# One transformer-like block on one core: Q/K rounding split, router steps, dt products, share of the C products on GpSimd, and new instruction orders

## The chip, the core and the metric

The kernel runs on one core of a Trainium2 chip. The core has TensorE (PE, matrix products, with its weight load shown apart as PEld), VectorE (DVE), ScalarE (ACT), GpSimd (POOL) and SyncE (SP, which here only issues transfers). Each engine takes its instructions strictly in the order in which they are written, and waits for another engine by a semaphore. The metric is the device time in microseconds; of the kernel before it is 5525.69 us, the median of 3 runs (5523.0 to 5528.63).

## The reference

32 batches of 512 tokens with 256 features go through an adaptive layer norm, a block, a second adaptive layer norm and a mixture of low-rank experts:

```python
h = layernorm(x) * (1 + ca) + sa
xn = ln(h, ln1);  q, k, v = xn @ q_w + q_b, xn @ k_w + k_b, xn @ v_w + v_b      # 16 heads of 16
attn_out = softmax(causal(q k^T / 4)) v @ o_w + o_b
x_ssm, z = split(xn @ in_proj_w)                                               # 512 and 512 features
x_c = silu(conv4(x_ssm) + conv_b);  dt_raw, Bm, Cm = split(x_c @ x_proj_w)      # 16, 16, 16
dt = softplus(dt_raw @ dt_w + dt_b)
# over t, for each of 512 channels and 16 states:  h = exp(dt*A)*h + (x_c*dt)*Bm ;  y = sum(Cm*h)
ssm_out = ((y + x_c*D_param) * silu(z)) @ ssm_out_w
x1 = h + a*attn_out + (1-a)*ssm_out;  x1 = x1 + gelu(ln(x1, ln2) @ ffn_w1 + b1) @ ffn_w2 + b2
x = x + ga * x1
h = layernorm(x) * (1 + cb) + sb
logits = h @ router_w.T + router_b                                             # 8 experts, the best 2 kept
w = softmax(where(logits < second_best, -1e9, logits))
x = x + gb * (h @ base_w.T + base_b + 2 * sum_e w_e * (h @ lora_A_e) @ lora_B_e)
```

## The kernel before, in words

One batch is one turn of a loop. In a turn each engine runs a list of named steps, and the five lists (ORDER, one for each engine) are written out by hand. A name with + belongs to the next batch, one with - to the batch before, so that three batches overlap. PLACE gives to each product of TensorE one of four PSUM banks (pM0 to pM3). A bank is filled again only when its last reader has signalled.

**The scan.** A batch has 64 scans (e = 0 to 63) of 128 channels by 512 tokens, in 32 pairs k. For each pair GpSimd writes x_c\*dt\*B into two of eight slots of `state` (step fill*k*, L575). ScalarE writes exp(dt\*A) into one of two PSUM banks pD (dec*e*, L714). VectorE scans (scan*e*, L1207). Then the result is multiplied by C: 48 of the 64 products on VectorE (c*e*, L1215, which reads pD and writes `state`), 16 on GpSimd (pc*e*, L563, which reads and writes `state`; for those the scan writes `state` instead of pD). The list POOL_C names the 16: both scans of each fourth pair. TensorE adds the product, transposed, into pY (add*e*, L945), and that frees the slot for a later fill. The rows of B and C come by transfers of SyncE (rb*k*, rc*k*) into four slots of `bc`; a row's transfer starts when the last reader of its slot has signalled.

**Attention.** TensorE makes scores (mx, L1033 and L1035), VectorE their row maxima (L1256), TensorE the scores again transposed with the maximum subtracted (st, L1051 and L1053), ScalarE the exponentials (L813), TensorE the product with V (pv, L967).

**Q and K in three bfloat16 parts.** Four chunks n of 128 by 512. TensorE makes the chunk in PSUM (qk*n*, L987). ScalarE rounds it plus its bias into the first part (L757). VectorE takes PSUM plus bias minus the first part into `qkf` (L1238). ScalarE rounds that into the second part (qm*n*, L762), GpSimd subtracts for the third (ql*n*, L603). SyncE stores the three parts. `qkf` is the same memory as `dbc`, one tile for all four chunks.

**dt.** Step xp (L1009, read by ScalarE at L782) leaves the 16 rows of dt_raw in rows 0 to 15 of `dbc`, B and C in the rows below. The four products dt*j* (L1014) use all 128 rows, with weights that are zero below row 15.

**Router.** VectorE adds the bias to the 128 by 4 by 8 logits from PSUM into `lg`, finds the 8 sorted values of each token (L1314) and sets `keep` in four small instructions (L1318). GpSimd subtracts the maximum (L631), ScalarE takes the exponential (L864), GpSimd multiplies with `keep` (L637), VectorE sums and inverts (L1321, L1323), GpSimd scales (L641), and VectorE weighs the low-rank product (lora, L1327).

## Time and profile before

| | |
|---|---|
| median of 3 runs | 5525.69 us (5523.0 to 5528.63) |
| the profiled execution | 5525.26 us, of which the span of its instructions is 5523.5 us |
| granted TensorE clock, mean | 0.985 (1.00 in the middle batches) |
| busy: PE, PEld | 5113.2 us (93%), 3450.1 us (62%) |
| busy: DVE | 4999.6 us (91%) |
| busy: ACT | 3967.2 us (72%) |
| busy: POOL | 4215.9 us (76%) |
| transfers | 812.22 MB, mean 147 GB/s; the main queue is in use 48.3% of the time of 16 engines |

Busy is the time in which an engine had at least one instruction in work; the rest of the span it was idle, and the profile names what ended each idle stretch. Products of TensorE overlap, so that the mean duration times the count exceeds its busy time. A turn of the loop shows the same pattern each time, so that one turn in the middle of the span stands for all but the first and the last.

### The profile page before, as it was taken

What the parts mean: (1) busy time and instruction counts of PE and PEld (TensorE: products, weight loads), DVE (VectorE), ACT (ScalarE), POOL (GpSimd) and SP (SyncE); (2) the same over time, 40 slices, a digit from 0 to 9 for tenths busy, and PEclk for the clock granted to TensorE, in tenths of its full rate; (3) what the DMA queues carried; (4) which work ended last, traced back from release to release, by engine and by line L of the source; (5) the groups of instructions that cost most, each with busy time, mean ns of one, the idle gap of its engine ahead of it and who ended that gap; (6) DMA issues with size and microseconds to landing.
All of it is one profiled execution on the core that took longest, in us unless ns stands there. A gap on an engine that the chain in (4) does not pass through costs nothing.

```text
span 5523.5 us, 94525 instructions
## 1 busy us (share of the span) xinstructions
PE 5113.2 (93%) x32280; PEld 3450.1 (62%) x32280; DVE 4999.6 (91%) x7745; ACT 3967.2 (72%) x6278; POOL 4215.9 (76%) x2641
## 2 busy tenths in 40 slices
PE   4799999999999999999999999999999999999996
PEld 2466666666666666666666666666666666666664
DVE  3999999999999999999999999999999999999983
ACT  2677777777777777777777777777777777777763
POOL 2778777887777887777877777888777888777772
PEclk7899999999999999999999999999999999999998
DMA  4444554444555454554444555444554445554440
GB/s 127 140 145 149 153 161 153 146 148 147 155 161 152 142 151 148 156 161 152 142 148 151 154 163 149 143 148 148 153 166 149 142 148 147 155 167 147 144 141 28
DMA packets 521455, 812.22 MB, mean 147 GB/s; under 512 B 80432, under 2 KB 227288, under 8 KB 520976
## 3 DMA queue, kind: packets, MB, share of 16 engines
q1 hardware_dynamic: 513072, 805.79, 48.3%
q8 instruction: 259, 4.24, 0.3%
q10 hardware_dynamic: 7904, 0.39, 0.1%
q14 instruction: 220, 1.80, 0.1%
HBM read 716.50 MB, written 88.38 MB: 146 GB/s over the span
## 4 chain that ended last, share of the span: by engine, by line
PE 44%; DVE 32%; issue 12%; ACT 5%; DMA 3%; POOL 1%; SPq 1%; ACTq 1%; DVEq 0%; POOLq 0%
DVE pD L1207 10%; DVE mx L1256 7%; PE pY L945 7%; PE pM L967 5%; DVE state L1207 4%; PE pM L1076 4%; DVE state L1215 4%; PE pM L1020 3%; DMA bc<-bc_d 3%; PE pM L1051 3%; DVE xc L1247 3%; PE pM L954 2%; PE pM L1002 2%; PE pM L1073 2%; PE pM L1125 2%
## 5 line engine op out<-in xcount | busy, mean ns | idle before, releaser
L575 POOL TENSOR_TENSOR state<-scan_in,bc 128x1024 f32<-128x1024 f32 x1024 | 2412.0, 2365 | 687.1 <-PE pY L945 439.6
L1207 DVE TENSOR_TENSOR_SCAN pD<-pD,state 128x512 f32<-128x512 f32 x1536 | 1849.0, 1217 | 76.3 <-POOL state L575 38.1
L714 ACT ACTIVATE pD<-scan_in,A 128x512 f32<-128x512 f32 x2048 | 1393.6, 688 | 584.0 <-DVE state L1215 482.3
L945 PE MATMUL pY<-ident,state 128*128 128x128 f32 x8192 | 1142.1, 276 | 12.1 <-POOL state L563 7.7
L945 PEld LDWEIGHTS pY<-ident,state 128*128 128x128 f32 x8192 | 912.1, 142 | 260.1 <-issue 172.5
L1215 DVE TENSOR_TENSOR state<-pD,bc 128x512 f32<-128x512 f32 x1536 | 1024.4, 681 | 42.1 <-DMA bc<-bc_d 27.7
L813 ACT ACTIVATE region<-pM 128x512 f32<-128x512 f32 (+1 forms) x1408 | 754.7, 555 | 327.9 <-PE pM L1053 292.5
L1256 DVE TENSOR_REDUCE mx<-pM 128x1 f32<-128x512 f32 (+3 forms) x1408 | 859.7, 630 | 130.0 <-PE pM L1035 127.8
L563 POOL TENSOR_TENSOR state<-state,bc 128x512 f32<-128x512 f32 x512 | 645.5, 1273 | 268.7 <-DVE state L1207 263.5
L1207 DVE TENSOR_TENSOR_SCAN state<-pD,state 128x512 f32<-128x512 f32 x512 | 611.5, 1210 | 78.2 <-ACT pD L714 78.2
L1033 PE MATMUL pM<-region 96*128 96x512 bf16 (+3 forms) x2048 | 527.9, 303 | 120.8 <-DVE mx L1256 73.6
L1051 PE MATMUL pM<-region 98*128 98x512 bf16 (+3 forms) x2048 | 533.1, 302 | 75.0 <-DVE mx L1256 40.4
L1087 PE MATMUL pM<-region,w_f 128*128 128x512 f32 x1024 | 455.3, 598 | 0.9 <-ACT region L845 0.9
L1096 PE MATMUL pM<-w_f,scan_in 128*128 128x256 f32 x2048 | 449.0, 380 | 5.7 <-ACT scan_in L854 5.7
L1096 PEld LDWEIGHTS pM<-w_f,scan_in 128*128 128x128 f32 x2048 | 387.7, 191 | 58.5 <-ACT scan_in L854 6.5
L1033 PEld LDWEIGHTS pM<-region 96*128 96x128 bf16 x2048 | 199.8, 98 | 314.1 <-issue 106.8
L1035 PE MATMUL pM<-mask_qk,identb 128*128 128x128 bf16 x2048 | 394.8, 220 | 0.0
L1053 PE MATMUL pM<-identb,mask_qk 128*128 128x128 bf16 x2048 | 392.2, 220 | 0.0
L967 PE MATMUL pM<-region,vt 128*17 128x512 f32 (+3 forms) x4096 | 369.0, 438 | 0.6 <-ACT region L813 0.6
L1051 PEld LDWEIGHTS pM<-region 98*128 98x128 bf16 x2048 | 199.1, 98 | 266.0 <-ACT region L813 124.0
L1087 PEld LDWEIGHTS pM<-region,w_f 128*128 128x128 f32 x1024 | 190.4, 191 | 218.2 <-issue 208.7
L1247 DVE SCALAR_TENSOR_TENSOR xc<-pM,conv_w,xc 128x511 f32<-128x511 f32 (+2 forms) x384 | 285.6, 744 | 22.1 <-ACT xc L774 13.1
(167 smaller groups left out, 8041.8 us busy)
## 6 DMA issues: line engine op xcount, KB each, us to landing
bc<-bc_d SPq DMA_DIRECT2D x2048, 256.0 KB, 4.0
region<-qk_d SPq DMA_DIRECT2D x640, 128.0 KB, 3.1
qk_d<-qkp SPq DMA_DIRECT2D x64, 384.0 KB, 3.5
qk_d<-ht SPq DMA_DIRECT2D x64, 384.0 KB, 2.7
xt<-in_x_dram SPq DMA_DIRECT2D x32, 512.0 KB, 5.2
region<-qk_d SPq DMA_DIRECT2D x256, 64.0 KB, 2.7
hres_d<-xt SPq DMA_DIRECT2D x32, 512.0 KB, 4.5
x<-hres_d SPq DMA_DIRECT2D x32, 512.0 KB, 5.5
```

Of the source, the lines that this page charges most:

```text
L563: nc.gpsimd.tensor_tensor(slot, slot, bc[:, e // JP % BC_SLOTS, 1, :], ALU.mult).then_inc(pp_ok.sem, 1)
L575: nc.gpsimd.tensor_tensor(state[:, at_:at_ + JP], us[:, parity(b), k // N * JP:(k // N + 1) * JP, :], bc[:, k % BC_SLOTS, 0, :].unsqueeze( ...
L714: act.activation(pD[DECAY_BANK[e]][:], dts[:, parity(b), j], ACT.Exp, scale=A[:, j, n:n + 1]).then_inc(a_ok.sem, 1)
L813: act.activation(probs[kb % 2][:, h:h + heads, 0:n], pM[bank_of(name)][:, 0:heads * n].rearrange("p (h t) -> p h t", h=heads), ACT.Exp, sc ...
L945: ins = pe.matmul(y_part(t, e % JP), state[:, e % RING, t * P:(t + 1) * P], ident[:], is_transpose=True, start=False, stop=(e % PASS >= PA ...
L1033: pe.matmul(ps[:, s * n:(s + 1) * n], q[0:QK_ROWS, h, qb * P:(qb + 1) * P], kk[0:QK_ROWS, h, 0:n], start=True, stop=False, skip_group_chec ...
L1051: pe.matmul(ps[:, i * n:(i + 1) * n], kk[0:QK_ROWS + 2, h + i, kb * P:(kb + 1) * P], q[0:QK_ROWS + 2, h + i, kb * P:L], start=True, stop=F ...
L1087: ins = pe.matmul(ps[:], w_f1[:, k, f * P:(f + 1) * P], h2T[:, k], start=(k == 0), stop=(k == KT - 1))
L1096: ins = pe.matmul(ps[:, t * D:(t + 1) * D], gT(b)[:, f, (2 * n + t) * P:(2 * n + t + 1) * P], w_f2[:, f, :], start=(f == 0), stop=(f == FT ...
L1207: v.tensor_tensor_scan(h if e in POOL_C else decay, decay, h, 0.0, ALU.mult, ALU.add)\
L1215: v.tensor_tensor(state[:, e % RING], pD[DECAY_BANK[e]][:], bc[:, slot, 1, :], ALU.mult)\
L1256: v.tensor_reduce(mx[:, g % 2].rearrange("p (h q) -> p h q", q=TB)[:, heads[0]:heads[-1] + 1, qb], pM[bank_of(name)][:, 0:len(heads) * n]. ...
```

## The change

- Router: all small steps but the exponential are on VectorE, and three of the four small tiles lie in the PSUM bank of the product, which is held until the last of them (`ew_ok`). The four instructions for `keep` are one, and one small memset goes.
- Q/K: ScalarE reads PSUM a second time and writes the unrounded chunk into `qkf`, and GpSimd subtracts the first part in place (new step qr*n*). VectorE has no part in it any more. ScalarE's second reading of chunk n waits until GpSimd is done with chunk n-1.
- dt: the weights and dt_raw lie in rows 0 to 15 and again in rows 64 to 79; the products of j = 0 and 2 use the first, those of 1 and 3 the second set of 16 rows. Two loads more stand at the start, one on SyncE, one on ScalarE.
- C products: GpSimd has 24 of 64, the 16 of before and e = 3, 11, 19, ... 59. Where the two products of a pair are on two engines, the next C row into their slot waits for both.
- All five orders and the bank numbers are new.

```diff
-POOL_C = [e for e in range(SCANS) if e // JP % 4 == 3]
+POOL_C = [e for e in range(SCANS) if e // JP % 4 == 3 or e % (4 * JP) == 2 * JP - 1]
...
+            parts = pM[bank_of("route")][:, 0:4 * TB * E].rearrange("p (c t e) -> p c t e", t=TB, e=E)
+            return parts[:, 0], parts[:, 1], parts[:, 2], parts[:, 3]
...
+            for row in (0, 64):
+                load(w_dt[row:row + R, :], d["dt_w"])
...
+                        if (JP * last in POOL_C) != (JP * last + JP - 1 in POOL_C):
+                            before.wait(sp, *product_after(JP * last))
                         before.wait(sp, *product_after(JP * last + JP - 1))
...
+                elif name[:2] == "qr":
+                    n = int(name[2])
+                    b.wait(pool, qk_f, n + 1)
+                    nc.gpsimd.tensor_tensor(qkf[:], qkf[:], qk_parts[n % 2][:, 0], ALU.subtract).then_inc(qk_r.sem, 1)
...
+                load(w_xp[:, :, 64:64 + R], d["x_proj_w"][:, 0:R].rearrange("(j p) n -> p j n", p=P))
...
+                    if n:
+                        b.wait(act, qk_lo, n)
+                    else:
+                        b.wait_last(act, dt_ps)
+                        b.wait_last(act, bc_out)
+                    act.activation(qkf[:], pM[bank_of(name)][:], ACT.Identity,
+                                   bias=qkv_b[:, n // 2, n % 2:n % 2 + 1]).then_inc(qk_f.sem, 1)
...
-                    pe.matmul(ps[:], w_dt[:, j * P:(j + 1) * P], dbc[:], start=True, stop=True)\
+                    half = slice(64 * (j % 2), 64 * (j % 2) + R)
+                    pe.matmul(ps[:], w_dt[half, j * P:(j + 1) * P], dbc[half], start=True, stop=True)\
...
-                    ps = next_bank(name, b, rt_c, 1, (h3_ok, KT))
+                    ps = next_bank(name, b, ew_ok, 1, (h3_ok, KT))
...
-                    for t in range(TB):
-                        v.tensor_scalar(keep[:, t, :], lg[:, t, :], top[:, t, 1:2], None, ALU.is_ge).then_inc(kp_ok.sem, 1)
+                    v.tensor_tensor(shifted, logits, top[:, :, 0:1].broadcast_to([P, TB, E]), ALU.subtract)\
+                     .then_inc(rk_ok.sem, 1)
+                    v.tensor_tensor(kept, logits, top[:, :, 1:2].broadcast_to([P, TB, E]), ALU.is_ge)\
+                     .then_inc(kp_ok.sem, 1)
                 elif name == "esum":
+                    _, kept, _, weighed = router_parts()
+                    b.wait(dve, ex_ok)
+                    v.tensor_tensor(weighed, kept, ew[:], ALU.mult).then_inc(wk_ok.sem, 1)
                     b.wait(dve, wk_ok)
-                    v.tensor_reduce(esum[:], ew[:], AX_X, ALU.add).then_inc(es_ok.sem, 1)
+                    v.tensor_reduce(esum[:], weighed, AX_X, ALU.add).then_inc(es_ok.sem, 1)
                     b.wait(dve, es_ok, 1)
                     v.reciprocal(esum[:], esum[:]).then_inc(es_ok.sem, 1)
+                    b.wait(dve, es_ok, 2)
+                    v.tensor_tensor(ew[:], weighed, esum[:].unsqueeze(2).broadcast_to([P, TB, E]), ALU.mult)\
+                     .then_inc(ew_ok.sem, 1)
...
     "POOL": """
-        fill7 fill8 +l0s fill9 pc14 pc15 +l0a fill10 +l0b fill11 +l0c fill12 pc22 +l1s fill13 pc23 -x2 -x2b fill14
+        fill8 fill9 +l0s pc14 pc15 -f1_0 +l0a +l0b pc19 fill10 +l0c fill11 +l1s fill12 pc22 fill13 pc23 -x2 -x2b
```

**First place: TensorE, the first of the dt products in a turn.** Before, it stands alone among scores, with a wait for a row maximum of VectorE (mx_ok); the next dt product comes 12 rows further down.

```order
L1051 MATMUL pM3<-region 128x512 [waits p_exp]
L1053 MATMUL pM3<-identb,mask_qk 128x128
L1033 MATMUL pM0<-region 128x384 [waits mx_ok]
L1035 MATMUL pM0<-mask_qk,identb 128x128
L1014 MATMUL pM0<-dbc,w_dt 128x512 [waits xp_ok,mx_ok]
L1033 MATMUL pM2<-region 128x384 [waits mx_ok]
L1035 MATMUL pM2<-mask_qk,identb 128x128
```

Now the same place:

```order
L1054 MATMUL pM1<-region 128x512 [waits xp_ok]
L1056 MATMUL pM1<-identb,mask_qk 128x128
L1017 MATMUL pM0<-dbc,w_dt 128x512 [waits xp_ok,mx_ok]
L1017 MATMUL pM2<-dbc,w_dt 128x512 [waits xp_ok,p_exp]
L1054 MATMUL pM3<-region 128x512 [waits mx_ok]
L1056 MATMUL pM3<-identb,mask_qk 128x128
```

The products of j = 0 and 1 now stand side by side, in two banks and two sets of rows. Those of j = 2 and 3 stand alone, among products over other sets of rows.

**Second place: GpSimd, from the gate of the block's output (L622, now L631) to the second ql step.** Before (`state<-scan_in,bc` is a fill, `state<-state,bc` a C product, `qkp<-dbc,qkp` and `ht<-dbc,ht` are ql steps, the ln rows the small steps of a layer norm):

```order
L563 TENSOR_TENSOR state<-state,bc 128x512
L622 TENSOR_TENSOR scan_in<-x,region 128x1024
L625 TENSOR_TENSOR region<-region,scan_in 128x1024
L575 TENSOR_TENSOR state<-scan_in,bc 128x1024
L543 TENSOR_TENSOR ln_rs<-ln_mv,eps 128x4
L544 TENSOR_TENSOR ln_nm<-ln_mv,mone 128x4
L546 TENSOR_TENSOR ln_rs<-ln_rs,mhalf 128x4
L549 TENSOR_TENSOR ln_nm<-ln_nm,ln_rs 128x4
L603 TENSOR_TENSOR qkp<-dbc,qkp 128x512
L575 TENSOR_TENSOR state<-scan_in,bc 128x1024 x2
```

Now (`dbc<-dbc,qkp` and `dbc<-dbc,ht` are the new qr steps):

```order
L634 TENSOR_TENSOR region<-region,scan_in 128x1024
L608 TENSOR_TENSOR dbc<-dbc,qkp 128x512
L580 TENSOR_TENSOR state<-scan_in,bc 128x1024
L612 TENSOR_TENSOR qkp<-dbc,qkp 128x512
L548 TENSOR_TENSOR ln_rs<-ln_mv,eps 128x4
L549 TENSOR_TENSOR ln_nm<-ln_mv,mone 128x4
L551 TENSOR_TENSOR ln_rs<-ln_rs,mhalf 128x4
L554 TENSOR_TENSOR ln_nm<-ln_nm,ln_rs 128x4
L608 TENSOR_TENSOR dbc<-dbc,ht 128x512
L568 TENSOR_TENSOR state<-state,bc 128x512
L580 TENSOR_TENSOR state<-scan_in,bc 128x1024 x2
L612 TENSOR_TENSOR ht<-dbc,ht 128x512
```

A qr step stands ahead of fill14, a second one and an added C product ahead of fill15 and fill16.

**Third place: VectorE, the router.** Before, a maximum, a C product and a Q/K step lie between the two halves, in which GpSimd and ScalarE do their parts:

```order
L1307 TENSOR_TENSOR lg<-pM,rb_row 128x32
L1312 MEMSET held 128x1
L1314 MAX top<-lg 128x8 x4
L1318 TENSOR_SCALAR keep<-lg,top 128x8 x4
L1256 TENSOR_REDUCE mx<-pM 128x2
L1256 TENSOR_REDUCE mx<-pM 128x4
L1215 TENSOR_TENSOR state<-pD,bc 128x512
L1238 SCALAR_TENSOR_TENSOR dbc<-pM,qkv_b,qkp 128x512
L1321 TENSOR_REDUCE esum<-top 128x4
L1323 RECIPROCAL esum<-esum 128x4
```

Now one maximum lies between them:

```order
L1299 TENSOR_TENSOR pM<-pM,rb_row 128x32
L1304 MAX top<-pM 128x8 x4
L1307 TENSOR_TENSOR pM<-pM,top 128x32
L1309 TENSOR_TENSOR pM<-pM,top 128x32
L1247 TENSOR_REDUCE mx<-pM 128x4
L1314 TENSOR_TENSOR pM<-pM,top 128x32
L1316 TENSOR_REDUCE esum<-pM 128x4
L1318 RECIPROCAL esum<-esum 128x4
L1320 TENSOR_TENSOR top<-pM,esum 128x32
```

## Rows read from the trace of the kernel before

**Rows 1.** Timeline of VectorE: the same gate step in two turns (start, us).

```profile
2702.29 1.27 DVE L1282 TENSOR_TENSOR zs<-zs,pY 128x512 f32<-128x512 f32 x2
...
2868.24 1.27 DVE L1282 TENSOR_TENSOR zs<-zs,pY 128x512 f32<-128x512 f32 x2
```

**Rows 2.** Busy time by stretch: PE, PEld, DVE, ACT, POOL, clock, DMA.

```profile
2684.00:2850.00 166.00, 158.02 (x1009) 106.86 (x1008) 155.75 (x242) 123.78 (x198) 131.55 (x82) 1.00 0.50 152
```

**Rows 3.** Waits of TensorE in 2684 to 2850: us, times, longest.

```profile
PE pM L1033 <- DVE mx L1256: 2.2, 2, 1.6
PE pM L1014 <- DVE mx L1256: 1.5, 2, 0.9
PE pM L1051 <- DVE mx L1256: 1.3, 3, 0.6
PE pM L1051 <- ACT region L813: 0.8, 1, 0.8
PE pM L1033 <- ACT region L831: 0.8, 1, 0.8
PE pY L936 <- DVE zs L1282: 0.5, 1, 0.5
```

**Rows 4.** The page's chain that ended last, by engine.

```profile
PE 44%; DVE 32%; issue 12%; ACT 5%; DMA 3%; POOL 1%; SPq 1%; ACTq 1%; DVEq 0%; POOLq 0%
```

**Rows 5.** Groups by line, whole span: busy us, mean ns, idle before, releaser.

```profile
L575 POOL TENSOR_TENSOR state<-scan_in,bc 128x1024 f32<-128x1024 f32 x1024 | 2412.0, 2365 | 687.1 <-PE pY L945 439.6 <-DMA bc<-bc_d 238.7
L1215 DVE TENSOR_TENSOR state<-pD,bc 128x512 f32<-128x512 f32 x1536 | 1024.4, 681 | 42.1 <-DMA bc<-bc_d 27.7
L563 POOL TENSOR_TENSOR state<-state,bc 128x512 f32<-128x512 f32 x512 | 645.5, 1273 | 268.7 <-DVE state L1207 263.5 <-DMA bc<-bc_d 4.7
L1238 DVE SCALAR_TENSOR_TENSOR dbc<-pM,qkv_b,qkp 128x512 f32<-128x512 f32 x64 | 47.4, 741 | 11.5 <-ACT qkp L757 11.5
L603 POOL TENSOR_TENSOR qkp<-dbc,qkp 128x512 bf16<-128x512 f32 x64 | 74.6, 1165 | 16.8 <-ACT qkp L762 16.8
L757 ACT ACTIVATE qkp<-pM,qkv_b 128x512 bf16<-128x512 f32 x64 | 44.0, 687 | 129.6 <-DMA qk_d<-qkp 73.4 <-PE pM L987 56.2
L1318 DVE TENSOR_SCALAR keep<-lg,top 128x8 f32<-128x8 f32 x128 | 23.0, 244 | 1.1
L1307 DVE TENSOR_TENSOR lg<-pM,rb_row 128x32 f32<-128x32 f32 x32 | 5.6, 176 | 10.5 <-PE pM L1107 10.5
L637 POOL TENSOR_TENSOR top<-top,keep 128x32 f32<-128x32 f32 x32 | 8.1, 253 | 28.1 <-ACT top L864 28.1
```

**Rows 6.** Timeline of TensorE: product with V, two scores, a dt product.

```profile
2713.06 0.22 PE L1035 MATMUL pM<-mask_qk,identb 128*128 128x128 bf16 x1
2713.21 1.05 PE L967 MATMUL pM<-region,vt 128*17 128x512 f32 x8
2714.19 0.66 PE L945 MATMUL pY<-ident,state 128*128 128x128 f32 x4
...
2716.40 0.22 PE L1033 MATMUL pM<-region 96*128 96x128 bf16 x1
2716.46 0.22 PE L1035 MATMUL pM<-mask_qk,identb 128*128 128x128 bf16 x1
...
2740.50 1.13 PE L1014 MATMUL pM<-dbc,w_dt 128*128 128x512 f32 x2 [0.87 <-DVE mx L1256]
2741.46 0.33 PE L1051 MATMUL pM<-region 98*128 98x384 bf16 x1
```

**Rows 7.** Waits of GpSimd in 2684 to 2850.

```profile
POOL state L575 <- PE pY L945: 12.4, 9, 3.2
POOL state L563 <- DVE state L1207: 8.5, 4, 4.0
POOL state L575 <- DMA bc<-bc_d: 7.9, 3, 5.9
POOL scan_in L622 <- DVE x L1298: 2.5, 1, 2.5
```

More of the change, by code:

```diff
@@ L984, in step @@
                     n = int(name[2])
-                    ps = next_bank(name, b, qk_r, n + 1, (xt_ok, KT))
+                    ps = next_bank(name, b, qk_f, n + 1, (xt_ok, KT))
                     for k in range(KT):
@@ L1228, in step @@
                     stats(b, 1, ht)
-                elif name[:2] == "qk":
-                    n = int(name[2])
-                    b.wait(dve, qk_hi, n + 1)
-                    if n:
-                        b.wait(dve, qk_lo, n)
-                    else:
-                        b.wait_last(dve, dt_ps)
-                        b.wait_last(dve, bc_out)
-                    v.scalar_tensor_tensor(out=qkf[:], in0=pM[bank_of(name)][:],
-                                           scalar=qkv_b[:, n // 2, n % 2:n % 2 + 1], in1=qk_parts[n % 2][:, 0],
-                                           op0=ALU.add, op1=ALU.subtract).then_inc(qk_r.sem, 1)
                 elif name in ("xs0", "xs1", "xs2", "xs3"):
@@ L1359 @@
+        ld0 -mt3 -rb30 -rc30 -rc29 -rc31 rb0 rc0 rc1 rb2 rb1 rb4 rc3 rb3 rc2 rb7 rb5 rc4 +load rb8 rb6 rc5 rb9 rc6
+        rc9 -xr rc7 rb11 rc8 rb10 ld1 rc11 rc12 rc10 rc13 rb13 rb12 mt0 rb14 rb16 ld2 rc14 rb15 +qk0 rc16 +l1a rb17
+        rc15 rb18 +qk1 x1p rc17 rc18 mt1 rb19 rb20 rb22 rc20 rb21 rc19 -put rc21 +qk2
     """,
     "POOL": """
-        fill7 fill8 +l0s fill9 pc14 pc15 +l0a fill10 +l0b fill11 +l0c fill12 pc22 +l1s fill13 pc23 -x2 -x2b fill14
-        -l3s +ql0 fill15 fill16 pc30 -xb +ql1 -route -wkeep fill17 -wnorm pc31 +ql2 fill18 fill19 -gb -put fill20
@@ L1363 @@
-        fill21 pc38 pc39 fill22 fill23 fill24 +ql3 fill25 pc46 pc47 fill26 fill27 fill28 fill29 pc54 pc55 fill30
-        fill31 +u0 +fill0 +u1 pc62 pc63 +fill1 +fill2 +fill3 +fill4 +pc6 +pc7 +fill5 l2s +fill6 f1_0
+        fill8 fill9 +l0s pc14 pc15 -f1_0 +l0a +l0b pc19 fill10 +l0c fill11 +l1s fill12 pc22 fill13 pc23 -x2 -x2b
+        +qr0 fill14 +ql0 -l3s +qr1 pc27 fill15 fill16 +ql1 fill17 pc30 +qr2 pc31 +ql2 fill18 -xb fill19 pc35 -gb
+        -put fill20 fill21 fill22 pc38 +qr3 pc39 pc43 +ql3 fill23 fill24 fill25 pc46 pc47 fill26 fill27 pc51 fill28
```

131 lines of the change are left out of this document (57 added, 74 removed).

## The prediction

> **What bounds the kernel now.** I read the timeline of VectorE first, for the length of a turn: the same gate step starts at 2702.29 and at 2868.24 us, so a batch takes 165.95 us [rows 1]. Thirty-two turns are 5310 us; the other 213 us of the span of 5523.5 are the setup, the half-filled first turn and the drain of the last. So the question is what one middle turn costs, times 32.
>
> Then the busy time by stretch, for a window as long as a turn [rows 2]: TensorE 158.0 of 166 us (95%), VectorE 155.75 (94%), GpSimd 131.55 (79%), ScalarE 123.8 (75%), at the full clock (1.00, the 2.4 GHz level). Two engines are nearly full and hand work to each other in a fixed order; neither alone is the bound. The transfers' engines are half busy. TensorE's idle 8.0 us then: the waits of the window name 7.1 of them, and 5.5 (2.2 + 1.5 + 1.3 + 0.5) end on VectorE, nearly all on a row maximum that comes late out of VectorE's queue; 1.6 end on ScalarE [rows 3]. The chain that ended last agrees: TensorE 44%, VectorE 32%, 12% hand-over between instructions, ScalarE 5%, GpSimd only 1% [rows 4]. GpSimd is off the path now; its idle time of 34 us a turn is mostly waiting for adds (12.4), scans (8.5) and rows of B (7.9) [rows 7].
>
> **The change, part by part, per turn.**
>
> VectorE. Eight C products go: busy 1024.4/1536 = 0.667 us each, -5.33. Four Q/K residuals go: 47.4/64 = 0.74 each, -2.96. Router: four `keep` instructions go (23.0/32 = 0.72) and a memset; added are four operations on 32 elements, for which the nearest row is the bias addition at 0.176: +0.70 against -0.78 [rows 5]. Sum -8.4: VectorE falls from 155.75 to 147.4 us.
>
> GpSimd. Eight C products come: 645.5/512 = 1.26 each, +10.1. Four qr steps, priced as the ql row of the same 128x512 (74.6/64 = 1.165), +4.7. Three router steps of about 0.25 go, -0.74 [rows 5]. Sum +14.0: from 131.55 to 145.6 us. The scans of the added eight write `state` at the same cost and free their pD bank one C product earlier, which helps ScalarE's decays; I count nothing for it, since ScalarE is not on the path.
>
> ScalarE. Four more readings of PSUM at 44.0/64 = 0.69: +2.75, to 126.5 us [rows 5]. It has 39 us to spare. What can hurt is its strict queue: the second reading of chunk n waits for the ql step of chunk n-1, and behind it stand decays and exponentials. Between qr0 and ql0 GpSimd has a fill (2.36 us [rows 5]), so ScalarE may stand for about 1 us there, four times a turn at worst; cost 0 to 4 us of ScalarE's 39, taken as 0 of the turn. If that cover is gone, decays come late to VectorE.
>
> TensorE, dt. A product over 128 rows by 512 columns is two records, 0.96 us from start to next start (2740.50 to 2741.46) [rows 6]. No row shows products on two sets of rows. The nearest is the product with V, four heads on four sets of output columns: eight records of 512 columns pass in 0.98 us (2713.21 to 2714.19), where eight at 0.48 would be 3.8 [rows 6]. So products on separate parts of the array do overlap almost fully, and one of the pair would be hidden: -0.96. Going in costs: the 128-column score ahead of it is followed after 0.15 us (2713.06 to 2713.21), where such a product is otherwise followed after 0.06 (2716.40 to 2716.46), so 0.09; with something for the way out I take 0.15 for a visit. Three visits a turn (the pair, j = 2, j = 3) are +0.45. Bounds: -0.96 (overlap, no switch) to +0.45 (switch, no overlap); I take -0.5, by the row of V.
>
> On this the Trainium skill speaks against the change in one point ("TensorEngine Tiling (Array Packing)", Key Properties): changing the tiling mode drains the TensorE; and "TensorE: Matmul & The Clock Gate", Part 3, says that a product with few rows takes as long as one with 128 and that the gain is in tiles running together. By the first alone j = 2 and j = 3 only lose, by the second the pair wins; the 0.09 us ahead of the product with V agree with a drain.
>
> Router, beyond its busy time: ScalarE's exponential (about 0.25 us) must return while VectorE does one maximum of 0.65; nearly hidden, 0 to 0.5, taken 0. TensorE holds the bank longer, until the weights are scaled; its next user is qk3, two steps later, so 0. SyncE: one wait more at eight C rows a turn, for a product that is as early or nearly as early as the one it waited for: 0. Start: two loads more, and in the first turn nothing covers Q/K; each of four chunks takes 0.69 + 1.17 instead of 0.74, +1.1. I take +3.5 us once for both (0 to 6).
>
> **The sum.** What does a turn gain? From below: VectorE's 32% of the chain are 53 us, and 8.4 of 155.75 (5.4%) of its work goes, 2.9; with dt 3.4 us. From above: all 5.5 us of TensorE's waits on VectorE go, and dt's 0.5: 6.0. GpSimd takes a part back. In its new list, from fill13 to fill20, stand seven fills, five C products, three qr, three ql and five steps of 128x1024: 16.5 + 6.3 + 7.0 + 11.8 = 41.6 us for seven pairs of scans, which at 162 us a turn last 35.4. Before it was 36.3 against 36.3 (7 x 165.95/32). GpSimd falls 6 us behind in this stretch and must have that lead; eight slots are four pairs, 20 us, less the 6 or so that a pair needs from fill to add. It should mostly hold. I take 3.9 us, near the lower value: a turn of 162.0. Times 32 that is -125; +3.5 at the start. 5525.3 - 125 + 3.5 = 5403.8 for the profiled execution, which lies 0.4 under the median of the runs: 5404 us.
>
> **Rivals.**
>
> A. TensorE becomes the only bound and runs nearly full. For it: with 147.4, 145.6 and 126.5 us all others have at least 10 us, and the waits on VectorE are the bulk. Against: order-bound waits do not vanish in the trace of any engine now. A turn of 159.0 (157.5 busy, 1.5 idle): 5525 - 222 + 3.5 = 5307 us.
>
> B. The freed time of VectorE turns into waiting. TensorE's 158.0 stay, and so does most of its idle time, now behind ScalarE or GpSimd. For it: VectorE already waits a few us a turn for others; against it, the maxima are what TensorE waits for most. A turn of 165.5: 5525 - 14 + 3.5 = 5514 us, at the edge of no change.
>
> C. Slower: GpSimd becomes the bound. Its waits are for adds and scans, inside a ring of eight slots, and a strict queue now also holds eight more waits for a scan and four for ScalarE. At 145.6 busy it may wait 20.4 us a turn before it is slower than now; it waits 34. If the waits for B rows (7.9) vanish but those for adds, scans and x1 stay (12.4 + 8.5 + 2.5 = 23.4 [rows 7]), a turn is 169.0: 5525 + 98 + 3.5 = 5627 us. For it: the stretch above. Against: waits for adds are waits of an engine that is ahead, and shrink as it falls behind; only the 8.5 for scans are of the other sort, and these scans come earlier.
>
> That dt's pair does not overlap is a rival inside the forecast: 0.96 x 32 = +31 us on it, 5435, less where VectorE hides it.
>
> **How the numbers follow.** Forecast 5404 with its own range 5335 to 5475 (a gain of 5.9 down to 1.6 us a turn): 0.62. A 0.12, B 0.12, C 0.14. What can be told from no change is 0.2%, 11 us: faster is under 5514.6, slower over 5536.7. Faster: 0.62 + 0.12 + half of B = 0.80; same 0.05 (of B); slower 0.14 of C and 0.01 of B = 0.15. The range leaves out C's far part and the best of A: 5315 to 5535.
>
> **What would show it.** Right: VectorE at 147 and GpSimd at 146 us in a turn; the sum of TensorE's waits on maxima cut by more than half, and by 1 us or more at dt; the second dt product of the pair starting under 0.1 us after the first; a turn of 160 to 164. GpSimd's waits for adds falling to a few us would show that it lives from its lead. Wrong: VectorE's waits for the fills of GpSimd grown to several us a turn (C); ScalarE's idle time ahead of its second Q/K reading over 2 us a turn with decays late behind it; TensorE waiting as before with other names (B); a busy time of dt that did not fall by some 0.9 us a turn.

## The result, and the profile after

The changed kernel takes 5300.28 us (median of 4 runs, 5297.9 to 5308.95) against 5526.03 us of the kernel before (4 runs, 5523.0 to 5528.63) on the same chip: ratio 0.9595, 95% interval 0.9581 to 0.961. That is 226 us faster; forecast were 5404 us and at best 5315. The profiled execution spans 5296.1 us.

A turn, by the same gate step of VectorE [rows 1 of before]:

```profile
2657.56 1.27 DVE L1273 TENSOR_TENSOR zs<-zs,pY 128x512 f32<-128x512 f32 x2
2816.30 1.27 DVE L1273 TENSOR_TENSOR zs<-zs,pY 128x512 f32<-128x512 f32 x2
```

This turn is 158.74 us, 7.2 less. It is one of the shortest: read at the same gate step over thirty turns, a turn is 158.73 to 160.04 us with a mean of 159.18, and 165.63 to 166.58 with a mean of 166.04 before. So the mean gain is 6.9 us a turn, 219.5 us in thirty-two turns, and what lies outside them is 202.3 us against 210.2 before, 8 us less. The forecast of 3.5 us more at the start can't be seen in this; the start alone was not measured.

Busy time in a window of a turn's length (PE, PEld, DVE, ACT, POOL, clock, DMA), against [rows 2]:

```profile
2684.00:2842.90 158.90, 156.85 (x1009) 106.02 (x1008) 148.81 (x228) 125.61 (x202) 144.94 (x92) 1.00 0.52 158
```

VectorE, GpSimd and ScalarE stand within 1.5 us of where the parts' sums put them (forecast 147.4, 145.6, 126.5). TensorE's idle time fell from 8.0 to 2.05 us, and its busy time by 1.2. Its named waits of the window, against [rows 3] (us, times, longest):

```profile
PE pM L1054 <- DVE mx L1247: 1.0, 1, 1.0
PE pM L1036 <- DVE xc L1238: 0.4, 1, 0.4
PE pM L1036 <- DVE mx L1247: 0.2, 1, 0.2
PE pM L1054 <- ACT region L815: 0.2, 1, 0.2
```

The waits on VectorE are 1.6 us (5.5 before), on ScalarE 0.2 (1.6 before). The chain that ended last, against [rows 4]:

```profile
PE 41%; POOL 16%; DVE 16%; issue 9%; ACT 9%; DMA 5%; SPq 2%; ACTq 1%; POOLq 0%; DVEq 0%
```

VectorE's share is halved, GpSimd's has gone from 1% to 16%. The groups that answer to [rows 5] (whole span: busy us, mean ns, idle before, releaser):

```profile
L580 POOL TENSOR_TENSOR state<-scan_in,bc 128x1024 f32<-128x1024 f32 x1024 | 2403.6, 2362 | 217.2 <-PE pY L947 159.6 <-DMA bc<-bc_d 53.8 <-issue 0.2
L568 POOL TENSOR_TENSOR state<-state,bc 128x512 f32<-128x512 f32 x768 | 972.5, 1276 | 135.6 <-DVE state L1210 130.2 <-DMA bc<-bc_d 2.7
L1218 DVE TENSOR_TENSOR state<-pD,bc 128x512 f32<-128x512 f32 x1280 | 861.1, 681 | 32.8 <-DMA bc<-bc_d 15.8
L608 POOL TENSOR_TENSOR dbc<-dbc,ht 128x512 f32<-128x512 f32 x64 | 74.4, 1162 | 2.4 <-ACT dbc L759 2.4
L759 ACT ACTIVATE dbc<-pM,qkv_b 128x512 f32<-128x512 f32 x128 | 87.7, 685 | 15.1 <-POOL qkp L612 14.6 <-POOL ht L612 0.5
L1307 DVE TENSOR_TENSOR pM<-pM,top 128x32 f32<-128x32 f32 x32 | 6.4, 199 | 1.1
```

The prices hold: C product on GpSimd 1.27, qr 1.16, second reading 0.69, a small router step 0.20 us (forecast 0.176). GpSimd's idle time before fills is 217 us in the whole run where it was 687; ScalarE stands 15 us in the whole run ahead of its second readings.

TensorE around the first dt products (start, us), against [rows 6]:

```profile
2781.23 0.22 PE L1056 MATMUL pM<-identb,mask_qk 128*128 128x128 bf16 x1
2781.38 1.32 PE L1017 MATMUL pM<-dbc,w_dt 16*128 16x512 f32 x4
2782.63 0.39 PE L1054 MATMUL pM<-region 98*128 98x512 bf16 x1
...
2785.86 0.22 PE L1056 MATMUL pM<-identb,mask_qk 128*128 128x128 bf16 x1
2786.01 1.12 PE L1017 MATMUL pM<-dbc,w_dt 16*128 16x512 f32 x2
2787.06 0.34 PE L1054 MATMUL pM<-region 98*128 98x384 bf16 x1
```

The pair takes 1.25 us, its way in 0.15 us instead of 0.06, so 0.09 for the way in. One alone takes 1.05 us; one over all rows takes 0.91 to 0.96 in the four places before, and 1.08 in this very place in e3 (below), so a cost of the way out is not shown.

Waits of GpSimd in the window, against [rows 7]:

```profile
POOL state L580 <- PE pY L947: 4.6, 2, 2.8
POOL state L568 <- DVE state L1210: 3.2, 3, 1.5
POOL ht L612 <- ACT ht L764: 2.1, 1, 2.1
POOL state L580 <- DMA bc<-bc_d: 1.9, 2, 1.2
```

Waits for adds fell from 12.4 to 4.6, for scans from 8.5 to 3.2, for B rows from 7.9 to 1.9: GpSimd used up its lead, and in this window neither TensorE nor VectorE waits for it.

### The profile page after: what moved, and what is told of

It is laid out like the page before. It is cut to its first block, busy times and chain, and to the rows that moved or that the text cites. A ratio compares the mean times of both kernels' runs of the same rounds, so it can differ in the third digit from the quotient of the medians.

```text
span 5296.1 us, 94529 instructions
## 1 busy us (share of the span) xinstructions
PE 5064.3 (96%) x32280; PEld 3416.3 (65%) x32280; DVE 4780.5 (90%) x7329; ACT 4024.5 (76%) x6406; POOL 4639.1 (88%) x2929
## 4 chain that ended last, share of the span: by engine, by line
PE 41%; POOL 16%; DVE 16%; issue 9%; ACT 9%; DMA 5%; SPq 2%; ACTq 1%; POOLq 0%; DVEq 0%
POOL state L580 8%; PE pY L947 7%; PE pM L1090 6%; PE pM L1099 6%; DVE pD L1210 5%; PE pM L1079 4%; DMA bc<-bc_d 4%; PE pM L1023 3%; DVE mx L1247 3%; PE pM L956 3%; DVE xc L1238 3%; DVE state L1218 2%; PE pM L1076 2%; DVE state L1210 2%; ACT pD L709 2%
## 5 line engine op out<-in xcount | busy, mean ns | idle before, releaser
L1210 DVE TENSOR_TENSOR_SCAN pD<-pD,state 128x512 f32<-128x512 f32 x1280 | 1547.7, 1218 | 155.9 <-ACT pD L709 146.5
L568 POOL TENSOR_TENSOR state<-state,bc 128x512 f32<-128x512 f32 x768 | 972.5, 1276 | 135.6 <-DVE state L1210 130.2
L947 PEld LDWEIGHTS pY<-ident,state 128*128 128x128 f32 x8192 | 899.8, 141 | 271.7 <-issue 148.4
L1210 DVE TENSOR_TENSOR_SCAN state<-pD,state 128x512 f32<-128x512 f32 x768 | 914.4, 1208 | 11.3 <-ACT pD L709 9.7
L1218 DVE TENSOR_TENSOR state<-pD,bc 128x512 f32<-128x512 f32 x1280 | 861.1, 681 | 32.8 <-DMA bc<-bc_d 15.8
```

Source lines behind the costliest of these rows:

```text
L568: nc.gpsimd.tensor_tensor(slot, slot, bc[:, e // JP % BC_SLOTS, 1, :], ALU.mult).then_inc(pp_ok.sem, 1)
L947: ins = pe.matmul(y_part(t, e % JP), state[:, e % RING, t * P:(t + 1) * P], ident[:], is_transpose=True, start=False, stop=(e % PASS >= PA ...
L1210: v.tensor_tensor_scan(h if e in POOL_C else decay, decay, h, 0.0, ALU.mult, ALU.add)\
L1218: v.tensor_tensor(state[:, e % RING], pD[DECAY_BANK[e]][:], bc[:, slot, 1, :], ALU.mult)\
```

## The experiments

All 18, in the order of the questions. "Old lists" are the orders and banks of the kernel before, "new lists" those of the changed kernel; the new router and the new dt products go with the new lists in every run but e3, where dt is as before. Ratios are to the kernel before on the same chip, with 95% intervals. A turn is read from the trace at the same gate step; a range is given where TensorE's clock falls in eight or more of thirty turns (below). The changed kernel is 5300.28 us, a turn of 158.74. e4 rests on two executions, the others on four or more.

| run | us | ratio | turn |
|---|---|---|---|
| e1 old lists, both moves | 5799.42 | 1.0501 (1.0483 to 1.0518) | 173.5 to 175.8 |
| e2 new lists, no move | 5537.06 | 1.002 (1.0011 to 1.0029) | 166.6 |
| e3 new, dt over all rows | 5302.19 | 0.9602 (0.9588 to 0.9616) | 158.7 |
| e4 new, TensorE +3.46 us | 5403.38 | 0.9783 (0.9763 to 0.9803) | 162.2 |
| e5 old lists, 24 C products | 5680.53 | 1.0282 (1.0267 to 1.0298) | 169.6 to 173.0 |
| e6 old lists, Q/K moved | 5617.98 | 1.0171 (1.0156 to 1.0187) | 169.2 |
| e7 new, 16 C products | 5387.99 | 0.9752 (0.9738 to 0.9767) | 161.75 |
| e8 new, Q/K on VectorE | 5438.38 | 0.9847 (0.983 to 0.9863) | 163.4 |
| e9 old lists, VectorE lighter | 5501.19 | 0.9958 (0.9945 to 0.9972) | 165.27 |
| e10 new, VectorE +3.3 | 5384.08 | 0.9746 (0.9733 to 0.9759) | 161.4 |
| e11 new, TensorE -3.45 (layer 1) | 5311.45 | 0.9612 (0.9599 to 0.9625) | 158.4 to 161.5 |
| e12 new, two dt pairs | 5302.02 | 0.9602 (0.9589 to 0.9615) | 158.8 |
| e13 as e11, GpSimd lighter | 5304.56 | 0.96 (0.9585 to 0.9614) | 158.4 to 160.7 |
| e14 new, VectorE, GpSimd lighter | 5285.98 | 0.9569 (0.9555 to 0.9583) | 158.6 |
| e15 all three lighter | 5291.58 | 0.9577 (0.9563 to 0.9592) | 158.3 to 160.8 |
| e16 old lists, TensorE +3.45 | 5633.57 | 1.0196 (1.0179 to 1.0213) | 169.5 |
| e17 new, TensorE -3.46 (layer 2) | 5322.45 | 0.9621 (0.9599 to 0.9644) | 158.9 to 162.6 |
| e18 as e17, others lighter | 5298.14 | 0.9588 (0.9573 to 0.9602) | 158.1 to 161.1 |

### Is it the split of the work or the lists? (e1, e2)

e1 is the kernel before with both moves (C products and Q/K) set into its old lists at the nearest places; e2 is the changed kernel with both taken back (cut to one line here; its lists on GpSimd and VectorE change to match).

```diff
 e1, GpSimd's old list (and c3, c11, ..., +qk0 to +qk3 out of VectorE's)
-        ... fill14 -l3s +ql0 fill15 fill16 pc30 -xb +ql1
+        ... fill14 +qr0 -l3s +ql0 fill15 fill16 +qr1 pc30 -xb +ql1
 e2, on the changed kernel
-POOL_C = [e for e in range(SCANS) if e // JP % 4 == 3 or e % (4 * JP) == 2 * JP - 1]
+POOL_C = [e for e in range(SCANS) if e // JP % 4 == 3]
```

> The kernel before with its own lists, banks, router and dt products; only the two moves of work are made: eight more C products on GpSimd and the Q/K residual by ScalarE and GpSimd, each new step set where the trace of before shows its input ready. VectorE falls by 8.3 us a turn, as in the changed kernel. Theory V (the relief of VectorE makes the gain, whatever the lists): TensorE's 5.5 us of waits on VectorE go, a turn of about 160.5, 5350 to 5380 us. Theory L (the new lists make it): the old lists hold the turn within 1 us of 165.95, 5495 to 5535 us. Both needed: in between or slower, 5400 to 5490, with TensorE idle under other names.

> The changed kernel with its lists, banks, router and dt pairs; the two moves of work are undone: 16 C products on GpSimd and the Q/K residual on VectorE, put into VectorE's new list where their inputs are ready. VectorE is back at about 156 us a turn. Theory V: the turn goes back to 164 or more, 5460 to 5530 us. Theory L: it stays within 1 us of 158.7, 5290 to 5335 us. Both needed: 5360 to 5450.

Neither half gains alone: the moves alone cost 275 us (5799.42 - 5524.35, the kernel before in these runs), the lists alone 13 us, both together win 226. Waits of TensorE in a turn of e1:

```profile
PE pM L1064 <- ACT region L826: 3.4, 2, 2.5
PE pY L958 <- POOL state L565: 2.5, 1, 2.5
PE pM L1046 <- DVE mx L1257: 2.2, 2, 1.6
PE pM L1027 <- DVE mx L1257: 1.5, 2, 0.9
PE pM L1000 <- ACT region L872: 1.5, 1, 1.5
PE pM L1064 <- DVE mx L1257: 1.3, 3, 0.6
```

VectorE has 7 us less to do there (148.4 busy), and TensorE waits for the row maxima exactly as long as before (2.2, 1.5, 1.3), and in addition for a C product of GpSimd and for ScalarE. Part of the 275 us is the clock: TensorE was at the half clock for 312 us of this execution, in the kernel before for 171. At half the speed the 141 us more cost up to 70 us, an estimate from these two figures. The places that I gave the added steps are one choice of many; better ones in the old lists may exist, and so may better places for the old split in the new lists: in e2 TensorE waits 2.6 us a turn for VectorE's Q/K residuals. The new router was never run without the new lists, so its own share is open; it stands in the 13 us of e2.

### Each move alone (e5, e6, e7, e8)

The same edits, one at a time.

> The kernel before with one move alone: 24 instead of 16 C products on GpSimd, each added one behind the scan that feeds it, by the trace of before. VectorE has 5.3 us less a turn, GpSimd 10.1 more. Both moves together in these lists gave 5799 us. Theory C (GpSimd's strict queue is what slows: the added products delay fills, the ring of eight slots runs empty): most of the loss is here, 5650 to 5800 us. Rival Q (the loss comes from the Q/K steps): no loss here, a gain from VectorE's relief, 5400 to 5530.

> The kernel before with the other move alone: the Q/K residual by ScalarE and GpSimd. VectorE has 3.0 us less a turn, GpSimd 4.7 and ScalarE 2.7 more. Theory C: 5500 to 5560 us, nearly no loss. Rival Q (ScalarE's second reading waits for a ql step that stands behind fills, and its decays and exponentials stand behind that): most of the loss is here, 5650 to 5800.

> The changed kernel with only the C products moved back: 16 on GpSimd, VectorE has 5.3 us more a turn (154.0). With both moves undone it is 5537 us. If VectorE's load is what counts, the loss of 237 us divides as 5.3 to 3.0: 5440 to 5460 us. If a mistimed Q/K residual was what cost in that kernel: 5300 to 5380.

> The changed kernel with only the Q/K residual back on VectorE, which has 3.0 us more a turn (151.5) and GpSimd 4.7 less. If VectorE's load counts: 5375 to 5400 us. If a residual that stands in VectorE's queue at a wrong time cost: 5430 to 5530. If TensorE still hides it: 5300 to 5320.

In the old lists each move loses (+156 and +93 us against 5524.9), in the new ones taking either back loses (+88 and +138 against 5300.3), and the two losses add up nearly to that of both (226 against 237). Taking the C products back costs 2.7 us a turn for 5.1 us of VectorE's work, 0.5 per us; taking Q/K back costs 4.3 us for 2.8. In e8 TensorE waits 1.7 us for VectorE's residual, which holds a bank:

```profile
PE pM L1025 <- DVE dbc L1230: 1.7, 1, 1.7
```

### What was VectorE's work worth before? (e9)

```diff
+                w = 32 if e % 8 == 3 or e % 16 == 9 else L
-                v.tensor_tensor(state[:, e % RING], pD[DECAY_BANK[e]][:], bc[:, slot, 1, :], ALU.mult)\
+                v.tensor_tensor(state[:, e % RING, 0:w], pD[DECAY_BANK[e]][:, 0:w], bc[:, slot, 1, 0:w], ALU.mult)\
```

> The kernel before with its old lists; 12 of the 48 C products of VectorE (e = 3, 11, ... 59 and 9, 25, 41, 57) run on 32 columns instead of 512, so that part of y is wrong. GpSimd, ScalarE and TensorE keep all their work. VectorE loses 12 x about 0.57 = 6.8 us a turn (155.7 to 149). It measures what VectorE's work alone is worth in the kernel before. Theory P, the working of my prediction (chain share 32%: 0.32 x 6.8 = 2.2 us): a turn of 163.8, about 5456 us, and with the rates 'from above' (all the 5.5 us of waits on VectorE) 160.5, 5350 us. Theory L (the old lists are timed for the old durations, so that what VectorE gives up is first of all waiting of its own for TensorE's scores, ScalarE's decays and GpSimd's fills): 0 to 1 us, 164.9 to 166.0, 5490 to 5527 us, with VectorE's idle time grown by 6 us. Theory T (TensorE with its own 158 us sets the turn and VectorE's lateness was nearly all that stood between): 159.5, 5320 us.

Busy time in a turn of e9:

```profile
2684.00:2849.30 165.30, 157.71 (x1009) 106.92 (x1008) 150.26 (x243) 123.68 (x196) 131.45 (x83) 1.00 0.51 152
```

TensorE's waits on maxima in the same window:

```profile
PE pM L1033 <- DVE mx L1257: 2.0, 2, 1.4
PE pM L1014 <- DVE mx L1257: 1.5, 2, 0.9
PE pM L1051 <- DVE mx L1257: 1.3, 3, 0.6
```

And VectorE's largest:

```profile
DVE mx L1257 <- PE pM L1035: 5.9, 9, 1.3
```

VectorE lost 5.5 us of work, the turn 0.7 (0.13 per us). TensorE's waits for maxima stay at 4.8 us of 5.0; VectorE's own waits for scores grew from 3.2 to 5.9. VectorE's freed time ends in its next wait, and this is theory L. It holds for work at these twelve places. Three of TensorE's waits (0.58, 0.65 and 0.87 us, at 2717.7 to 2729.9 us) come after a stretch of VectorE's list in which all C products (e = 44, 45, 48, 49) keep their 512 columns; the short product ahead of it, e = 43, only lengthened VectorE's wait for ScalarE's `xc` from 0.2 to 0.7 us. The lists of e1 and e5 keep the same four there. What a lighter VectorE inside that stretch would give was not run. The page "Perfetto Trace Analysis" of the Trainium skill (Optimization Strategies) advises to work on the engines that block the critical path while TensorE waits; VectorE was 32% of that chain, by which 5.5 us of its work would be worth 1.8 us; relieving it alone gave 0.7.

### More and less work, engine by engine (e4, e16, e10, e11)

e4 and e16 add four products of the ffn's first layer to TensorE in the new and the old lists, e10 five C products into a spare tile to VectorE, e11 cuts the first layer by the same amount.

```diff
 e4, e16
+                    if f % 2 == 0:
+                        pe.matmul(ps[:], w_f1[:, 0, f * P:(f + 1) * P], h2T[:, 0], start=True, stop=True)
 e10
+                if e in (8, 20, 32, 44, 56):
+                    v.tensor_tensor(spare[:], pD[DECAY_BANK[e]][:], bc[:, slot, 1, :], ALU.mult)
 e11 (and the stop flag of the last product to match)
-                    for k in range(KT):
+                    for k in range(1 if f % 2 == 0 else KT):
```

> The changed kernel with four products of 128x512 more in the first feed-forward step, each done twice for every second tile, two records of 0.43 us each: TensorE has 3.45 us more a turn, no other engine has more. Theory M (TensorE is the only bound now): the turn grows by all of it, +110 us, 5400 to 5415. If the turn is set by the play of several engines: half of it or less hides in waits, 5330 to 5365.

> The kernel before, old lists, with four extra products of 128x512 over 128 rows in the ffn's first layer, 3.45 us more of TensorE's work a turn, result unchanged. Theory H (the old turn of 165.95 is TensorE's work plus waits that do not depend on it): +3.4 us a turn, 5635 us, the full rate as in the new lists. Theory K (TensorE's 8 us idle take a part of it, since the waits are for VectorE, which has the same time as before): +1 to +2.4 us a turn, 5557 to 5602 us.

> The changed kernel with five extra C products a turn into a spare tile on VectorE (ahead of e = 8, 20, 32, 44, 56): 5 x 0.66 = 3.3 us of VectorE work a turn, result unchanged. VectorE goes from 148.8 to 152.1 busy of 158.8. Theory T (TensorE alone bounds the new lists): VectorE has 10 us idle and the turn grows by 0 to 1 us, 5300 to 5332 us. Theory V (VectorE and TensorE still bound together, VectorE by its old 32% of the chain or more): +1.1 to +3.3 us a turn, 5335 to 5406 us. For comparison, 3.46 us more of TensorE's work made the turn 3.46 us longer, at the full rate.

> The changed kernel with four of the eight ffn_w1 products (f = 0, 2, 4, 6) over one of their two halves of the features: 8 records less, 3.45 us less of TensorE's work a turn; that part of the ffn's output is wrong. The mirror of the run with 3.45 us more, which cost all of it. Theory T (TensorE is the only bound, and the others have 10 to 30 us to spare): the turn falls by 2.5 to 3.45 us, to 155.4 to 156.3, 5190 to 5220 us. Theory N (the next bound is close: the chain of the changed kernel gives GpSimd 16% and VectorE 16%): the fall is 1 us or less, 5268 us or more, with GpSimd's or VectorE's waits no smaller and TensorE's idle time grown by 2 us or more. What lies between says how far the next bound is.

TensorE's added 3.46 us cost nearly all of themselves, in the new lists (+103 us, 3.2 a turn) and in the old ones (+109, 3.4). VectorE's cost 2.6 of 3.3 us. But 3.45 us less on TensorE gives nothing; the mirror is broken. The trace of e11 shows where most of it went: TensorE stands 2.0 us for ScalarE's readings, in the very place of the cut.

```profile
PE pM L1090 <- ACT scan_in L852: 2.0, 2, 1.4
PE pM L1054 <- DMA region<-mrow: 1.2, 1, 1.2
PE pM L1054 <- DVE mx L1247: 1.0, 1, 1.0
```

So "TensorE is the only bound", which I had read from e4 alone, falls.

A second part went to the clock. The same two waits stand in e15 (next section), which has the same cut. In ten of its thirty turns TensorE's granted clock falls right behind them to the lower of its two levels (1.2 GHz, shown as 0.50, where the full 2.4 GHz is 1.00) for 3.4 us. Two rows of TensorE's timeline, and the busy times of the stretch behind:

```profile
617.10 1.12 PE L1092 MATMUL pM<-region,w_f 128*128 128x512 f32 x2 [0.55 <-ACT scan_in L854]
619.64 3.50 PE L1092 MATMUL pM<-region,w_f 128*128 128x512 f32 x4 [1.42 <-ACT scan_in L854]
620.10:623.40 3.30, 3.30 (x7) 1.35 (x6) 1.92 (x2) 1.47 (x4) 3.22 (x2) 0.50 0.60 186
```

These ten turns take 160.3 us in the mean, the twenty at full clock 158.7. In the thirty turns of the changed kernel the clock never falls. It falls for 38 us of thirty turns in e11, 27 in e13, 102 in e17 and 72 in e18; in the last two it does so behind a wait of mostly 2.6 us, in e1 behind one of 2.5. The longest wait of TensorE in a turn of the kernel before is 1.6 us, and its clock falls in two of thirty turns.

### Which second bound? (e13, e14, e15, e17, e18)

The chain of e11 ran from the router through GpSimd's stretch up to fill20 and on to VectorE, so I lightened these (theory E: that chain is the second bound): six C products of GpSimd in that stretch and twelve of VectorE on 32 columns. e17 cuts TensorE in the ffn's second layer instead, where it runs without a wait (theory W: only ScalarE's readings in the first layer ate the cut; theory M: something else is as long as TensorE's work).

```diff
 e13, e14, e15, e18: GpSimd (e14, e15, e18 also VectorE, with e % 8 == 1 or e % 16 == 4)
+                w = 32 if e in (14, 15, 19, 22, 23, 27) else L
 e17, e18 (and the stop flag to match)
-                        for f in range(FT):
+                        for f in range(FT - 2):
```

> The changed kernel with two things lighter: TensorE's four shortened ffn_w1 products as before (-3.45 us a turn), and six C products of GpSimd (e = 14, 15, 19, 22, 23, 27, all in the stretch after the router) on 32 columns instead of 512, 6 x about 1.1 = 6.6 us a turn. Parts of the ffn's output and of y are wrong. Theory E (two cycles of equal length: TensorE's own work, and the one through that stretch of GpSimd): now both are shorter and the turn falls by 2 to 3.4 us, to 155.3 to 156.8, 5185 to 5235 us. Theory G0 (GpSimd is not in the second cycle, its share of the chain only stands beside others' work): as with less of TensorE alone, 158 to 160, 5285 to 5315 us.

> The changed kernel with GpSimd's six C products as in the run above and twelve C products of VectorE (e = 1, 9, ... 57 and 4, 20, 36, 52) on 32 columns: 6.6 us less on GpSimd, about 6.8 us less on VectorE; parts of y are wrong; TensorE has all its work. Theory E and theory T (TensorE's own work is one of the bounds): its idle time of 2.1 us at most can go, so the turn is 157 to 158.7, 5245 to 5300 us. Theory O (TensorE is never a bound by itself, it only follows the others): the turn falls by 3 us or more, under 5205 us, which TensorE's busy time of 157 would contradict.

> The changed kernel with all three lighter: TensorE -3.45 us, GpSimd -6.6 us, VectorE -6.8 us a turn, as in the two runs above; the same parts of the output are wrong. TensorE's busy time is then 153.5. Theory E: 154.5 to 155.5 a turn, 5160 to 5195 us, and if it is clearly below the run with less of TensorE and GpSimd alone, VectorE's stretch belongs to the second cycle too. Theory M (a third bound of the same length lies elsewhere, in ScalarE's order or the transfers of B and C rows): 157.5 or more, 5260 us or more.

> The changed kernel with the ffn's second layer over six of its eight blocks of features: 16 of 64 records less, 16 x 0.216 = 3.46 us less of TensorE's work a turn, in a place where nothing is waited for; part of the ffn's output is wrong. Theory W (TensorE sets the turn wherever ScalarE does not pace it, and the cut in the first layer was lost only to ScalarE's readings there): -2.5 to -3.46 us a turn, 155.3 to 156.2, 5190 to 5220 us. Theory M (a second bound as long as TensorE's, whose path does not run through this place): 158.0 to 158.7, 5278 to 5300 us, with TensorE's waits grown by about 3 us at other names. In between: the distance to that second bound.

> The kernel of the run above, with VectorE's twelve and GpSimd's six C products on 32 columns too (about 6.8 and 6.6 us less a turn); parts of the ffn's output and of y are wrong. Theory W with nothing else near: as above, within 0.5 us a turn of it. If the run above gains little and this one 2.5 us or more a turn (5220 us or less), the second bound is VectorE's and GpSimd's work. If neither gains (5265 us or more), ScalarE or the transfers hold the turn at 158 as well.

The most that any of them wins is 14 us (e14, 0.3%). The lower clock does not hide a larger gain: the shortest turns at full clock are 158.4 us in e11 and e13, 158.3 in e15, 158.9 in e17 and 158.1 in e18, against 158.7 in the changed kernel. Theories E and W fall; M holds: something else ends at nearly the same time. The waits of e17 and e18 name one such thing. TensorE in a turn of e18, with 2.6 us for ScalarE's `ht` (the normalised input of the next batch, L716 of the changed kernel):

```profile
PE pM L958 <- ACT ht L718: 2.6, 1, 2.6
PE pM L1056 <- DVE mx L1250: 0.8, 1, 0.8
PE pM L1038 <- DVE xc L1241: 0.4, 1, 0.4
```

And the same stretch of ScalarE in the changed kernel itself:

```profile
2698.20 0.67 ACT L852 ACTIVATE scan_in<-pM,f_b 128x512 f32<-128x512 f32 x1
2698.89 1.28 ACT L856 ACT_TABLE_LOAD   x1
2700.19 3.62 ACT L856 ACTIVATE scan_in<-scan_in 128x4096 f32<-128x4096 f32 x1
2703.83 1.28 ACT L709 ACT_TABLE_LOAD   x1
...
2706.95 1.28 ACT L805 ACT_TABLE_LOAD   x1
2708.25 1.91 ACT L805 ACTIVATE zs<-zs 128x2048 f32<-128x2048 f32 x1
2710.18 1.28 ACT L709 ACT_TABLE_LOAD   x1
...
2715.35 2.06 ACT L716 ACTIVATE ht<-ht,ln_nm,ln_rs 128x256 f32<-128x256 f32 x4
```

From the last reading of the first layer to the end of `ht` at 2717.41 ScalarE has 19 us with 1.1 us of gaps: gelu, silu, four table loads (5.1 us), six decays. TensorE comes for `ht` at 2718.13, 0.7 us later. A cut of 3.46 us of TensorE's work inside this stretch can win 0.7 at this place, and the 2.6 us wait is the rest. The turns of e18 agree: at full clock they take 158.1 us at the shortest, 0.6 less than 158.7, and the 21 of thirty with a fall of the clock behind that wait take 159.9 in the mean, so that the 0.6 is gone in the time of the run. ScalarE, busy 125.6 of 158.9 us, sets the pace of a stretch though not of the turn. That its stretch is the bound was argued from these waits; no run made ScalarE lighter. In e17 even the 0.6 is missing (158.9), and I have not followed why; the traces of e11 and e17 also show about 1 us of waits for the transfer of `mrow` that the changed kernel lacks.

### The dt products (e3, e12)

e3 is the changed kernel with all four dt products over all 128 rows, e12 has dt3 moved up to dt2, so that two pairs stand side by side.

```diff
 e3
-                    pe.matmul(ps[:], w_dt[half, j * P:(j + 1) * P], dbc[half], start=True, stop=True)\
+                    pe.matmul(ps[:], w_dt[:, j * P:(j + 1) * P], dbc[:], start=True, stop=True)\
 e12, TensorE's list
-        ... st2_1_2 +dt2 st2_1_3 st2_2_0 add49 ... pv2_2 +dt3 add50
+        ... st2_1_2 +dt2 +dt3 st2_1_3 add49 st2_2_0 ... pv2_2 add50
```

> The changed kernel with the dt products over all 128 rows as before, in the new places. If TensorE alone sets the turn, its time follows TensorE's work: from the changed kernel's trace the pair saves 0.67 us and three visits cost 0.1 to 0.2 each, so 0.1 to 0.5 us a turn more, 5303 to 5316 us. If the pair does not matter (TensorE is not the bound): within 3 us of 5300. If the way in and out costs more than the pair saves: faster, 5280 to 5297.

> The changed kernel with dt3 moved up right behind dt2 (TensorE: st2_1_2 dt2 dt3 st2_1_3 add49 st2_2_0; ScalarE reads dt2, the exponentials of st2_1_3, then dt3; dt2 in bank 0, dt3 in bank 1), so that the four dt products are two pairs on two sets of rows and not one pair and two alone. From the rows of the changed kernel: a pair takes 1.25 us and 0.15 to come in, one alone 1.05 and 0.15; two alone 2.40, a pair 1.40, so 1.0 us a turn of TensorE's time goes. Theory T (TensorE is the only bound): -0.6 to -1.0 us a turn, 5268 to 5281 us. Theory N (the banks and ScalarE's order cost as much there, st2_2_0 waiting for ScalarE's reading of dt2): no change within 0.2%, 5290 to 5311 us.

In e3 the same two products side by side take 1.77 us (4 records):

```profile
2784.49 1.93 PE L1014 MATMUL pM<-dbc,w_dt 128*128 128x512 f32 x4
2786.26 0.38 PE L1051 MATMUL pM<-region 98*128 98x512 bf16 x1
```

So the overlap is real, 0.52 us less for this pair. Over all four products the changed kernel takes 3.35 us and 0.18 for two slower ways in, e3 3.82, so dt gains 0.3 us a turn. In e12 the second pair takes no longer than one product alone (1.06 against 1.05 us), the first again 1.25; why the first is slower is open.

```profile
2787.99 1.13 PE L1017 MATMUL pM<-dbc,w_dt 16*128 16x512 f32 x4
2789.05 0.34 PE L1054 MATMUL pM<-region 98*128 98x384 bf16 x1
```

Neither run can be told from the changed kernel (+1.9 and +1.7 us), though e12 takes 1.0 us off TensorE's busy time of a turn (155.7 against 156.6, mean of the turns): one more cut that wins nothing. The row pairs are worth nothing that can be measured here, and none of the 18 runs beats the changed kernel with the whole computation.

## Why the prediction was wrong

**Right.** The busy time of VectorE, GpSimd and ScalarE within 1.5 us, though VectorE's fell by 6.9 and not by 8.4; the prices of the new operations; the signs "waits on maxima cut by more than half" (5.0 to 1.2) and "waits for adds falling to a few us"; no wait for fills on VectorE, so C did not come, and e13 and e14 show no gain of note from a lighter GpSimd.

**Wrong: the step "What does a turn gain?"** I set bounds of 3.4 and 6.0 us and took 3.9. Measured are 7.2 in the turn shown and 6.9 in the mean, above both. By the windows of a turn, the 7.2 are made up of these:

| part of the gain, us a turn | before | now | gain |
|---|---|---|---|
| TensorE's waits on VectorE | 5.5 | 1.6 | 3.9 |
| its waits on ScalarE | 1.6 | 0.2 | 1.4 |
| its idle time that no wait names | 0.9 | 0.25 | 0.6 |
| its busy time | 158.0 | 156.85 | 1.2 |

That the forecast of 3.9 equals the measured fall of VectorE's waits is luck: it was taken near a share of the chain, and holds 0.5 for dt. What it missed are the terms that it put at nothing: ScalarE's waits, the unnamed idle time, and a fall of TensorE's busy time beyond dt. That fall is not dt's: e3, with dt over all rows, has 156.2 us in its window, and e2, with the row pairs, 158.05 of 166.6; e10, which adds nothing to TensorE's work, has 158.05 of 161.4. Why TensorE's busy time is longer in the slower turns is open.

Three things in the working failed.

The lower end priced VectorE's 8.4 us by its 32% share of the chain. A share says where the last chain ran, not what a microsecond there is worth: e9 measured 0.13 per us in the old lists, e10 0.8 and e7 0.5 in the new ones. The lower end's own rate, 2.9 for 8.4, is 0.34. None of the three is that, and the kernel with both moves in the old lists is 275 us slower.

The upper end let go only TensorE's waits on VectorE (5.5 us). But the lists are new for all engines, and 1.4 us of the 1.6 on ScalarE went too, and most of the rest that no wait named. I treated the new lists as a detail of the moves. They are the other half of the change: worth nothing alone (e2), and without them the moves are a loss, at the places tried (e1).

"GpSimd takes a part back" rested on 41.6 us of GpSimd's work for 35.4 us of scans in one stretch. The lead held: GpSimd's waits for adds and scans shrank to 7.8 us, and in e14 GpSimd and VectorE together 6.6 and 6.8 us lighter win 0.45 us a turn.

By the working's own sum the ends of the range, 5335 and 5475, belong to a gain of 6.1 and 1.7 us a turn, and not of 5.9 and 1.6; the measured time lies outside either way.

**Dt, -0.5.** The overlap was 0.52 us for the pair and not 0.96: about -0.3 in all against e3, and nothing in the time. The sign of being wrong, that dt's busy time did not fall by some 0.9 us, came true: 0.4. "The second starts under 0.1 us after the first" can't be read from rows that join both; the pair's 1.25 us show that it overlaps in part, and the 1.06 of e12's second pair that it can overlap in full. The Trainium skill's rule ("TensorEngine Tiling (Array Packing)", Key Properties) that changing the tiling mode drains TensorE agrees with the 0.09 us of the way in. The sentence on products with few rows, which the prediction places in Part 3 of "TensorE: Matmul & The Clock Gate" of the Trainium skill, stands there under "Why this matters for your kernels"; the trace agrees, 1.05 us for 16 rows and 0.91 to 1.08 for 128.

**Rival A** (turn 159.0, 5307 us, chance 0.12) came true in its numbers: 158.74 and 5300. In its mechanism it is half right. TensorE's work counts nearly in full when it grows, but it did so before as well (e16), and it is not the only bound: VectorE's counts 0.8 when it grows, and hardly anything wins when TensorE's shrinks.

What the runs show instead: the split and the lists gain only together, and the time of a turn is set by how the five lists fit the durations. In the old lists TensorE has 8 us of waits that stand at fixed places and mostly stay when VectorE gets lighter. In the new lists TensorE's own 157 us and ScalarE's stretch up to `ht` lie within 0.7 us of each other, and more work costs at once, while less wins 0.6 us a turn at most, even at full clock. Even with TensorE, VectorE and GpSimd all lighter a turn at full clock stays at 158.3 (e15). That ScalarE's order is what holds it there is the likely reading and was not tested.
